# Where the low half of the second layer norm's x is computed: VectorE or GpSimd

## What is computed

```
mod = silu(c) @ w_mod + b_mod
sh_msa, sc_msa, g_msa, sh_mlp, sc_mlp, g_mlp = split(mod, 6)
xn = ln(x) * (1 + sc_msa) + sh_msa
q, k, v = split(xn @ w_qkv + b_qkv)            # 16 heads of 18; layers 0 and 2 norm q and k per head
o = softmax(q @ k.T / sqrt(18)) @ v
x = x + g_msa * (o @ w_proj + b_proj)
xn2 = ln(x) * (1 + sc_mlp) + sh_mlp
h = gelu(xn2 @ w1 + b1)                        # 288 -> 1152
x = x + g_mlp * (h @ w2 + b2)
```

## Time and profile before

| what | us |
|---|---|
| median of 3 runs | 4670.65 |
| lowest and highest of them | 4670.15 and 4674.21 |
| the profiled execution | 4671.22 |
| its span in the trace | 4669.4 |
| PE busy in the span | 4205.1 (90%) |
| DVE busy | 3631.2 (78%) |
| ACT busy | 2303.7 (49%) |
| POOL busy | 1093.6 (23%) |

### The profile page before, as it was taken

One profiled execution on the slowest core, in us unless ns is written; L12 is line 12 of the kernel. 1 busy time (PEld: TensorE's weight loads), 2 busy tenths in 40 slices (PEclk: granted clock), 3 DMA queues, 4 the chain that ended last, 5 costly groups with the idle time before them and its releaser, 6 DMA issues. The chain is left out here.

```text
span 4669.4 us, 124471 instructions
## 1 busy us (share of the span) xinstructions
PE 4205.1 (90%) x46073; PEld 3567.4 (76%) x46073; DVE 3631.2 (78%) x7659; ACT 2303.7 (49%) x3894; POOL 1093.6 (23%) x2045
## 2 busy tenths in 40 slices
PE   6754899999999995999999999975999999999998
PEld 4543688888888874888888888864888888888886
DVE  5665888888988874777777777756888888888884
ACT  1112555555555543555555555534555555555553
POOL 1001222222222222222222222221222222222221
PEclk7576999999999997999999999997999999999999
DMA  3001111110111111111101111011011011110100
GB/s 77 22 0 46 36 28 30 30 30 25 29 30 30 30 30 52 29 30 30 30 24 30 30 30 30 24 38 48 22 29 27 24 31 25 26 27 24 31 24 19
DMA packets 122230, 141.58 MB, mean 30 GB/s; under 512 B 14447, under 2 KB 117781, under 8 KB 122113
## 3 DMA queue, kind: packets, MB, share of 16 engines
q1 hardware_dynamic: 121968, 139.75, 11.3%
q10 hardware_dynamic: 144, 0.22, 0.0%
HBM read 110.87 MB, written 29.06 MB: 30 GB/s over the span
## 5 line engine op out<-in xcount | busy, mean ns | idle before, releaser
L870 DVE TENSOR_REDUCE mx<-S 128x4 f32<-128x1024 f32 x768 | 903.1, 1218 | 180.9 <-PE S L1104 173.4
L630 ACT ACTIVATE pT<-S 128x1024 f32<-128x1024 f32 x768 | 745.4, 1022 | 376.1 <-PE S L1132 375.7
L578 ACT ACTIVATE hf<-M 128x512 f32<-128x512 f32 (+1 forms) x480 | 267.0, 556 | 732.5 <-DVE hl L861 378.7
L507 POOL TENSOR_SCALAR hh<-hf 128x512 fp32r<-128x512 f32 (+1 forms) x480 | 280.3, 584 | 821.9 <-ACT hf L578 783.3
L1132 PE MATMUL S<-qT,kT 32*128 32x256 f32 x9216 | 426.9, 296 | 45.9 <-ACT pT L630 42.5
L1145 PE MATMUL A<-pT,V 128*32 128x256 f32 x6144 | 415.1, 388 | 26.3 <-ACT pT L630 26.3
L1132 PEld LDWEIGHTS S<-qT,kT 32*128 32x128 f32 x9216 | 330.0, 185 | 118.1 <-ACT pT L630 70.4
L1184 PE MATMUL M<-xh,w_hi 128*128 128x256 f32 x1728 | 363.6, 291 | 3.5 <-POOL xh L483 3.5
L1039 PE MATMUL A<-wqkv_hi,xh 128*128 128x288 f32 x1152 | 284.6, 329 | 87.1 <-DVE x L917 79.5
L1223 PE MATMUL M<-w_lo,hh 128*128 128x288 f32 x1728 | 350.5, 304 | 0.0
L1184 PE MATMUL M<-xh,w_lo 128*128 128x256 f32 x1728 | 343.5, 280 | 0.0
(11 more groups left out here) (231 smaller groups left out, 9915.4 us busy)
## 6 DMA issues: line engine op xcount, KB each, us to landing
mid<-xbo SPq DMA_DIRECT2D x64, 288.0 KB, 4.0
xld<-mid SPq DMA_DIRECT2D x64, 288.0 KB, 3.1
xa<-mid SPq DMA_DIRECT2D x64, 288.0 KB, 3.6
gA<-gates SPq DMA_DIRECT2D x96, 144.0 KB, 3.3
gM<-gates SPq DMA_DIRECT2D x96, 144.0 KB, 3.6
xld<-in_x_dram SPq DMA_DIRECT2D x32, 288.0 KB, 3.9
xa<-in_x_dram SPq DMA_DIRECT2D x32, 288.0 KB, 3.5
out_dram<-xbo SPq DMA_DIRECT2D x32, 288.0 KB, 2.2
```

Of the source, the lines that this page charges most:

```text
L507: pool.tensor_scalar(hh[:, 2 * f:2 * f + m, :].rearrange("p m c -> p (m c)"), hf[:, f % 3, 0:m * T], 1.0, 0.0, ALU.mult, ALU.add).then_inc ...
L578: act.activation(hf[:, f % 3, 0:c], MBANK[f % 2][:, 0:c], ACT.Gelu if rot else ACT.Gelu_apprx_tanh).then_inc(s["m_hf"], 1)
L630: act.activation(pT[:, g % 2, 2 * h:2 * h + 2, :], S[:, 2 * h:2 * h + 2, :], ACT.Exp, scale=float(HD) ** -0.5).then_inc(s["a_ex"], 1)
L870: dve.tensor_reduce(mx[:, p, :, :], S[:, r:r + 2, :].rearrange("p a (t k) -> p a t k", t=NT), AX.X, ALU.max).then_inc(s["a_mx"], 1)
```

## The change

The two subtractions leave DVE and are made by POOL, directly behind the three roundings and ahead of the copies into `V`. Each of the two now signals `m_xl` itself, so its count for a run goes from 1 to 2, and POOL waits for its own rounding ahead of the first, for the first ahead of the second, and for the second ahead of what follows. PE and ACT wait for the count of 2.

```
-    ... m_xl=1 ...
+    ... m_xl=2 ...
 POOL
+                    def M_xl(n):
+
+                        wait(pool, "m_xh", n, 3)
+                        constant_wait(pool)
+                        pool.tensor_tensor(xl2[:, :, :], xf2[:, 0:FULL, :], xh2[:, :, :].bitcast(F32), ALU.subtract).then_inc(s["m_xl"], 1)
+                        wait(pool, "m_xl", n, 1)
+                        pool.tensor_tensor(xm2[REST:2 * REST, :], xf2[REST:2 * REST, FULL, :], xm2[REST:2 * REST, :].bitcast(F32), ALU.subtract).then_inc(s["m_xl"], 1)
+                        wait(pool, "m_xl", n, 2)
...
                             M_xh(m)
+                            M_xl(m)
                         if p is not None:
                             A_v(p)
 ACT, M_gelu
-                            wait(act, "m_xl", n, 1)
+                            wait(act, "m_xl", n, 2)
 DVE
-                    def M_xl(n):
-                        wait(dve, "m_h", n, 0)
-                        wait(dve, "m_xh", n, 3)
-                        low_x(xf2, xh2[:, :, :], xl2[:, :, :], xm2).then_inc(s["m_xl"], 1)
...
-                        if m is not None:
-                            M_xl(m)
 PE, M_up_part
-                                wait(pe, "m_xl", n, 1)
+                                wait(pe, "m_xl", n, 2)
```

More of the change, by code:

```diff
@@ L50 @@
     a_pr=2, a_prd=2, a_xa=16, a_x1=2, a_warm=2,
-    m_g=16, m_bn=2, m_st=1, m_ve=1, m_rs=1, m_xn=2, m_gb=1, m_xb=1, m_xT=2, m_xf=3, m_xh=3, m_xl=1, m_h=5,
+    m_g=16, m_bn=2, m_st=1, m_ve=1, m_rs=1, m_xn=2, m_gb=1, m_xb=1, m_xT=2, m_xf=3, m_xh=3, m_xl=2, m_h=5,
     m_hf=5, m_hh=5, m_hl=5, m_y=2, m_x2=2, m_out=16, m_mod=1, a_mod=1,
```

## The result

The changed kernel takes **4681.6 us**, the median of 15 runs (4678.29 to 4684.1); the kernel before took 4672.22 us in the same comparison (15 runs, 4667.27 to 4674.44). The ratio is 1.0021, 95% interval [1.0013, 1.0029]: slower, and by the 0.2% at which a difference of this kernel begins to show. The forecast was 4681 us.

The account below looks back on a forecast made before the run. The prediction took a loop from PE's transposes through DVE's second reciprocal and low halves to PE's scores as the bound. 0 + 5.4 + 4.4 = 9.8 us on 4671.22 us gave a median of 4681 us, range 4673 to 4691.

Parts of the forecast that it names:

- What bounds the kernel: Loop from PE's transposes through DVE's second reciprocal, small copies and low halves to PE's scores; lines 794 and 795 stand ahead.
- What leaves DVE: 1.25 and 0.41 us a slot leave DVE ahead of the second reciprocal, which PE holds back; gain counted as nothing.
- The prices on POOL: The subtractions on POOL take 1275 ns for `xl2` and 742 ns for `xm2`, with waits of 0.15, 0.08 and 0.31 us.
- The collision, 0.06 us a slot: POOL's later copies into `V` hold up DVE's small copies, making `qT` and the slot 0.06 us later, 5.4 us in all.
- The exclusion: POOL and certain DVE instructions lock shared SBUF ports, so line 898 waits for the copies into `V`; if wrong, 5.4 us becomes 0.
- The ends of the layers, 4.4 us: In each layer's last two slots, without run p, PE starts 0.44 and 1.02 us late; three layers make 4.4 us.
- The sum: 0 + 5.4 + 4.4 = 9.8 us on the profiled execution of 4671.22 us, the median lying 0.57 us lower.
- the loop's term: The delay of DVE's small copies by POOL's copies into `V`, 0.06 us in each of 90 slots, 5.4 us.

Follow-up runs that it names:

- v_late: The changed kernel with POOL's copies into `V` moved behind the second rounding of the gelu's output; 4698.39 us, ratio 1.0058 to the kernel before.
- x_early: The kernel before with the first residual's first product (line 917) put ahead of two low halves of the gelu's output on DVE; 4613.69 us, ratio 0.9873.
- no_low: The kernel before with the two subtractions left out on every engine, `xl2` being constant zero; 4665.38 us, ratio 0.9986.
- best: The changed kernel with first low halves and first residual product earlier, last two slots' subtractions on DVE, `V` copies behind the fourth gelu rounding; 4607.39 us.
- before_best: The kernel before with first low halves of q and k ahead of the reciprocals and the first residual product ahead of two gelu low halves; 4604.72 us.
- ends_pool: The kernel before, but POOL makes the two subtractions in the two slots of a layer with an MLP and no run p; 4680.38 us, ratio 1.0015.
- ends_dve: The changed kernel, but the two subtractions stay on DVE in the two slots of a layer with an MLP and no run p; 4675.66 us, ratio 1.0008.
- v_first: The changed kernel with POOL's copies into `V` put ahead of the two subtractions; 4686.56 us, ratio 1.0031 to the kernel before.
- v_free: The changed kernel with POOL's copies into `V` moved behind the fourth rounding of the gelu's output; 4677.39 us, ratio 1.0010 to the kernel before.
- lo_early: The changed kernel with the first low halves of q and k put ahead of the reciprocals on DVE; 4668.6 us, ratio 0.9986 to the kernel before.

## Why the prediction was right, and where its sizes were off

- **What bounds the kernel.** Right: v_late lost and x_early won in DVE's stretch from the second reciprocal to line 917, no_low won no slot ahead of it. One thing was missed in the stretch from the reciprocals to the low halves, which the prediction read as running without a gap. The idle time is indeed small (0.02 us between the reciprocals), but the order there is not the shortest: the pair takes 0.18 us less when the second is not held back by PE. It did not touch this change, whose work stands ahead of both, but it hid a gain of 0.3%.
- **What leaves DVE is worth nothing.** Right, shown by no_low and by best against before_best. The second reciprocal stands 0.03 to 0.04 us behind the transposes in the kernel before, in the change and in no_low.
- **The prices on POOL.** Right nearly to the hundredth. Lines 489 and 491 of the kernel after (ns, least, median, longest):

```profile
L489 POOL TENSOR_TENSOR xl<-hf,xh x96: 1267/1277/1283, 523.0 to 4642.8; 128x512 fp32r<-128x512 f32 x96
...
L491 POOL TENSOR_TENSOR xm<-hf,xm x96: 715/728/735, 524.3 to 4644.1; 32x256 fp32r<-32x256 f32 x96
```

  1275 and 742 ns were forecast; the waits in the slot shown are 0.15, 0.08 and 0.31 us, as forecast. With the rate of "GPSIMD Engine Reference" of the Trainium skill, section "Elementwise — side-by-side cycle accounting", in place of the rows' 2.08 ns a column, the first would have been 809 + 224 x 2.17 = 1295 ns, an estimate; the rows stood nearer.
- **The collision, 0.06 us a slot.** The mechanism was right, its size was not: 0.030, 0.008 and 0.015 us in the three layers, 1.6 us in place of 5.4. This is the mis-sized term. Counted from the second reciprocal, it had the copies into `V` end at 1.33 us and `qT` start 0.07 us behind them, after the earlier trace rows; in the slot shown they end at 1.30 us (1131.34 - 1130.04), and `qT` starts 0.06 us behind. Over 27 slots of layer 0, and counted from the transposes, `qT` starts 0.04 us later than in the kernel before, but the last low half of k ends only 0.03 us later: the low halves between give 0.01 us back, which the forecast did not have. In layers 1 and 2 that last end is 0.013 and 0.019 us later, which is about what their slots lose. In layer 1 the reason lies in the kernel before, where `qT` starts 0.016 us later than in layer 0; in layer 2 the copies into `V` end 0.012 us earlier.
- **The exclusion.** The page "SBUF — State Buffer" of the Trainium skill, section "Who interferes with whom", had GpSimd and a VectorE instruction with two SBUF inputs, or a copy in a two-port mode, lock each other out. The runs agree: small copies 0.41 us beside the copies into `V`, 0.38 without; a low half 0.90 beside a rounding, 0.69 without; and the scaled output, with one input in PSUM, keeps its 0.82 us beside the copies into `V`.
- **The ends of the layers, 4.4 us.** The waits were right: the slot before the last is 0.40 to 0.43 us longer (0.44 forecast), PE's wait in the last grew by 1.56 - 0.57 = 0.99 us (1.02 forecast). What failed is that nothing else would follow. In the profile the clock fell in two of the three waits, and the layer changes cost 2.1 and 3.4 us, while the third gave 0.5 us back, together 6.3 us; over all kernels the ends cost 6.0 us. The waits alone make 4.2 of that (1.2 us in the slots before the last, three times 0.99). The other 1.8 us were not accounted for one by one; the falls of the clock are the likeliest source, but that is argued, not shown.
- **The sum.** 9.8 us were forecast, 9.4 measured between medians, but the terms were forecast for the profiled execution, and that grew by 7.7 us. There the loop's term was 3.8 us too large and the ends' 1.9 us too small. That the forecast of 4681 us met the median of 4681.6 is luck in part: two errors cancelled by half, and the rest lies in the spread of the runs.

## What to carry to other kernels

Freed time on a busy engine is worth something only behind the last wait that this engine shares with the loop: 1.66 us a slot ahead of the second reciprocal were worth nothing, 0.2 us behind it 18 us, and an order that let one product go first 60 us. A stretch without idle time can still be too long: two short instructions that follow each other freely overlap (0.36 us for both), and lose that when the second is held back (0.54 us). A row that groups them shows it by its length alone. Work moved to a slower engine must also be costed where the pipeline drains, since there nothing covers it.

## What the runs showed that was not expected

- **The granted clock at the ends of the layers.** In the last slot it fell to 0.50 for 6.6 to 6.8 us in and behind a wait of some 1.56 us for POOL (the change, ends_pool), for some 3 us about one of 0.58 us for DVE (ends_dve), and not at all behind the same 0.57 us in the kernel before. Nor did it in layer 0 of v_first, whose PE waited as long as the change's (PE's timeline, then busy times and granted clock from before the end of that wait):

```profile
1763.48 0.50 PE L1188 MATMUL M<-xl,w_hi 128*128 128x256 f32 x2 [1.56 <-POOL xm L491]
```

```profile
1762.00:1766.00 4.00, 2.52 (x21) 2.53 (x22) 0.00 (x0) 0.60 (x1) 1.34 (x2) 1.00 0.00 0
1766.00:1772.00 6.00, 5.75 (x46) 5.45 (x46) 2.82 (x3) 3.47 (x6) 5.65 (x7) 1.00 0.01 1
```

  So the wait alone does not decide it. Over all traces such a fall comes in 9 of 18 last slots with POOL's subtractions, and then lasts 6.8 us, and in 12 of 21 with DVE's, and then lasts 3.4 us. In layer 0 the time from the last slot to the next layer is 135.7 to 135.9 us with POOL's subtractions and a fall (the change, ends_pool, v_late), 133.4 to 134.9 us without one (v_free, v_first, lo_early). What decides whether the clock falls stays open, and with it some 1 to 2 us at a change of layers, by these figures of layer 0.
- **Exclusion reaches plain roundings.** A POOL instruction with a single input (line 516 in v_late), which lay over the first 0.37 us of a VectorE subtraction with two inputs, made it 0.21 us longer.
